# Loads of x and stores of the output rows in 112 and 15 partitions, or one strided transfer of 128 rows, in place of 127

## The chip, the cores and the metric

The kernel runs on one core of one Trainium2 chip. A core has TensorE (PE; PEld is its weight loading), VectorE (DVE), ScalarE (ACT), GpSimd (POOL) and SyncE (SP), on-chip memories SBUF and PSUM with 128 partitions each, and 16 DMA engines that move data between SBUF and the chip's main memory. The metric is the device time of one execution in microseconds, as the median of several runs. Lower is better.

## The reference, cut to what matters

```python
xn = layernorm(x)                                  # x: 6250 nodes x 256, f32; src, dst: 200000 edges
h = relu(xn[dst] @ W1 + b1); w = sigmoid(h @ W2 + b2)
gnn = segment_sum(xn[dst] * w, src) / segment_sum(w, src)
k, v = head_norm(xn, kln), head_norm(xn, vln)      # 8 heads of 32
mix = einsum(q=xn, kv=k.T @ v / N) + xn
x = x + gnn + mix
f = layernorm(x)
top2 of softmax(relu(f @ r1) @ r2) over 6 experts, each a 3-layer MLP of 256
return x + sum(top2 weight * expert(f))            # out_rows: 6250 x 256, f32
```

## The kernel before, in words

The 6250 nodes are laid out as 49 blocks (`BLOCKS`): node 49p + b is lane (partition) p of block b. 6250 is no multiple of 49, so lanes 0 to 126 (`LANES` = 127) have all 49 blocks and the last lane has only 27 (`SHORT`). In main memory the 49 rows of a lane lie side by side, 49 KB; the rows of one block lie 49 rows apart.

Opening. SyncE issues every plain DMA, from one queue in program order: first the edge arrays src and dst (125 partitions of 1600), then x in two parts (`X_PARTS`: blocks 0 to 20, blocks 21 to 48), each as a DMA of 127 partitions and one for the last lane (lines 494 to 498; part 1 behind a wait for VectorE's memset of the missing rows, `x_zeroed`), then 13 small weights and biases (L500 to L512) and six more. VectorE builds one sort key for each edge and runs a bitonic sort of 18 levels over them (L1399, L1407). Between its early passes it computes the statistics of x (L1369, L1373), part 0 after level 2, part 1 after level 3; it waits for `x_loaded[part]` there. GpSimd turns the statistics into scale and shift (L621 to L627). ScalarE then normalises blocks (L772, waiting for all small loads, x_loaded[0] and x_norm) and TensorE, ScalarE and GpSimd run 25 front rounds of two blocks each, in which GpSimd has the spread (L639 to L647). From level 8 on the sort needs TensorE's transposes (L1089); front rounds are placed between them.

Dense loop. After the sort a loop over the blocks builds for each destination block the counts of its edges by source (VectorE's one-hot marks, L1475; TensorE L1130; ScalarE's copy L927) in groups, two groups ahead, and multiplies them with the table of normalised rows (TensorE L1148). In the same round, spread over 28 steps, the six experts of the block two behind are computed (TensorE L1173, L1182, L1190; ScalarE L887), and the next block is normalised and routed. VectorE starts the output row block `y_acc` with L1586 in step 3 and adds one expert each time with L1593, the last in step 27. There is one `y_acc`. `store_all` on SyncE waits for the last add of block b, then stores it: for b < 27 with a DMA of lanes 0 to 126 and a second of the last lane, from 27 on with the first alone and a `nop` that adds the other 16 to `row_stored`. L1586 of the next block waits for `row_stored`, because it overwrites `y_acc`:

```python
if experts and j == places["begin"]:
    dve.wait_ge(S["row_stored"], 1 + 32 * n)
    dve.wait_ge(S["b3_ps"], n + 1)
    nc.vector.tensor_tensor(y_acc, x2, ps_b3, ALU.add)
```

VectorE executes in order, so whatever mark (L1475) comes behind L1586 waits with it. The last two blocks run without the building of counts (`ALONE`). A second path (`cut_flag`) repeats the aggregation in another way; it is not taken with these inputs.

Of the kernel before, what the change touches and what calls it, by code (L numbers as in the profile page):

```python
# [24 lines left out]
P = 128  # L25
NODES, DIM = 6250, 256
# [9 lines left out]
BLOCKS = -(-NODES // P)  # L36
# [3 lines left out]
LANES = NODES // BLOCKS  # L40
SHORT = NODES - LANES * BLOCKS
assert LANES == P - 1 and 0 < SHORT < BLOCKS

# [165 lines left out]
def gps_layer(nc, a, out, y_table, kept_keys):  # L211
    with ExitStack() as ctx:
# [7 lines left out]
        base = sb("base", [P, BLOCKS, DIM])  # L220
# [109 lines left out]
        x2, xn2, y_acc = after(DIM), after(DIM), after(DIM)  # L330
# [107 lines left out]
        S = {name: sem(name) for name in names}  # L438
# [38 lines left out]
        ordered = keys[exchanges_before(LEVELS + 1, LEVELS) % 2]  # L477
        assert ordered.shape == keys[1].shape

        node_rows = [t[0:LANES * BLOCKS, :].rearrange("(p t) d -> p t d", t=BLOCKS) for t in (a["x"], out)]  # L480
        last_rows = [t[LANES * BLOCKS:NODES, :].unsqueeze(0) for t in (a["x"], out)]
        kept_chunks = kept_keys[0:COLS, :].rearrange("(t p) q -> p t q", p=P)
        ordered_chunks = ordered.rearrange("p (t q) -> p t q", q=P)

# [3 lines left out]
        def _(sp):  # L488
# [2 lines left out]

            (at, to), (rest_at, rest_to) = X_PARTS
            assert to <= SHORT < rest_to
            sp.dma_start(base[0:LANES, at:to, :], node_rows[0][:, at:to, :]).then_inc(x_loaded[0], 16)
            sp.dma_start(base[LANES:P, at:to, :], last_rows[0][:, at:to, :]).then_inc(x_loaded[0], 16)
            sp.wait_ge(S["x_zeroed"], 1)
            sp.dma_start(base[0:LANES, rest_at:rest_to, :], node_rows[0][:, rest_at:rest_to, :]).then_inc(x_loaded[1], 16)
            sp.dma_start(base[LANES:P, rest_at:SHORT, :], last_rows[0][:, rest_at:SHORT, :]).then_inc(x_loaded[1], 16)

            sp.dma_start(gnn_w1[:, :, :], a["L0_gnn_W1"].rearrange("(h p) n -> p h n", p=P)).then_inc(S["small_loaded"], 16)  # L500
            sp.dma_start(gnn_b1[:, :], a["L0_gnn_b1"].rearrange("(p o) -> p o", o=1)).then_inc(S["small_loaded"], 16)
# [42 lines left out]
            def store_all(first):  # L544
                with sp.Fori(0, SHORT) as b:
                    sp.wait_ge(S["ey_added"], 1 + EXPERTS * (first + b + 1))
                    sp.dma_start(node_rows[1][:, bass.ds(b, 1), :], y_acc[0:LANES, :].unsqueeze(1)).then_inc(S["row_stored"], 16)
                    sp.dma_start(last_rows[1][:, bass.ds(b, 1), :], y_acc[LANES:P, :].unsqueeze(1)).then_inc(S["row_stored"], 16)
                with sp.Fori(SHORT, BLOCKS) as b:
                    sp.wait_ge(S["ey_added"], 1 + EXPERTS * (first + b + 1))  # L550
                    sp.dma_start(node_rows[1][:, bass.ds(b, 1), :], y_acc[0:LANES, :].unsqueeze(1)).then_inc(S["row_stored"], 16)
                    sp.nop().then_inc(S["row_stored"], 16)
                sp.wait_ge(S["row_stored"], 1 + 32 * (first + BLOCKS))

            store_all(0)
# [195 lines left out]
        def _(act):  # L751
# [9 lines left out]
                act.wait_ge(S["dst_lane_ready"], n + 1)  # L761
                nc.scalar.activation(dst_lane, dst_lane, ACT.Identity, bias=shift[0:LOAD_ROWS, :]).then_inc(S["dst_lane_ready"], 1)
            act.wait_ge(S["small_loaded"], 16 * N_SMALL)
            act.wait_ge(x_loaded[0], 32)
            act.wait_ge(S["x_norm"], 1)


# [44 lines left out]
            with nc.scalar.Fori(*FRONT_FIRST) as u:  # L812
                front_round(u)

            act.wait_ge(x_loaded[1], 32)
            act.wait_ge(S["x_norm"], 2)


# [482 lines left out]
        def _(dve):  # L1301
# [59 lines left out]

            def statistics(part):
                at, to = X_PARTS[part]
                dve.wait_ge(x_loaded[part], 32)
                dve.wait_ge(S["x_zeroed"], 1)
                per = 7
                with nc.vector.Fori(at // per, to // per) as t:
                    for k in range(per):
                        nc.vector.bn_stats(x_stats[:, per * t + k, :], base[:, per * t + k, :]).then_inc(S["x_stat"], 1)  # L1369

                dve.wait_ge(S["x_stat"], to)
                for t in range(at, to):
                    nc.vector.bn_aggr(x_mean_var[:, t, :], x_stats[:, t, :]).then_inc(S["x_stats_ready"], 1)  # L1373
# [364 lines left out]
```

## Time and profile before

| | us |
|---|---|
| median of 3 runs | 2786.89 (2786.73 to 2791.58) |
| profiled execution, own time | 2783.34 |
| its span on the core | 2781.6 |
| TensorE busy | 2196.4 (79%) |
| VectorE busy | 1760.5 (63%) |
| ScalarE busy | 1157.1 (42%) |
| GpSimd busy | 494.1 (18%) |
| DMA moved | 30.83 MB, mean 11 GB/s |

In the profile, times are microseconds from the start of the span, unless marked ns. A slice digit is the busy share in tenths of one fortieth of the span (70 us), 9 for 90% or more; PEclk is the TensorE clock granted, in tenths of 2.4 GHz, so that 5 is its lower level of 1.2 GHz. The chain that ended last is followed back from the last instruction: at each step to what released it. "SPq" is an issue on SyncE's queue. A stretch of the windows view lists the busy time of each engine in it with the number of instructions, then the granted clock, the mean busy share of the 16 DMA engines and what they moved.

### The profile page before, as it was taken

To read this page: it belongs to the slowest core of one execution; us is meant where nothing else is said; L and a number is where in the kernel's file an instruction comes from. 1 tells how busy PE (TensorE), PEld (TensorE's weight loads), DVE (VectorE), ACT (ScalarE), POOL (GpSimd) and SP (SyncE) were. 2 spreads that over 40 slices of the span, in tenths; PEclk is the share of its full clock that TensorE was granted. 3 is DMA by queue.
4 is the path that set the end of the run, shared out by engine and by line. 5 is a ranking of instruction groups with operands and counts; after the bars stand their busy time and mean duration, and the time that the engine had idled before them with its cause. 6 is when DMAs were issued, how large, how long until landed. Compare 5 with 4: busy or idle time off the path is not lost.

```text
span 2781.6 us, 53408 instructions
## 1 busy us (share of the span) xinstructions
PE 2196.4 (79%) x18096; PEld 1961.3 (71%) x18096; DVE 1760.5 (63%) x4212; ACT 1157.1 (42%) x2861; POOL 494.1 (18%) x414
## 2 busy tenths in 40 slices
PE   0002477654499999999999999999999999999997
PEld 0001366644388888888888888888888888888886
DVE  4203489899686666566666666666666666666662
ACT  0001234324444544444444454544445445444444
POOL 0001967778710000000000000000000000000000
PEclk9999677757699999999999999999999999999999
DMA  1000000001120000000000000000000000000000
GB/s 44 27 29 23 0 0 1 1 10 46 52 72 5 5 5 6 5 4 6 5 4 6 5 4 5 6 5 4 6 5 4 6 5 4 5 6 4 4 5 7
DMA packets 29005, 30.83 MB, mean 11 GB/s; under 512 B 7283, under 2 KB 26852, under 8 KB 28703
## 3 DMA queue, kind: packets, MB, share of 16 engines
q1 hardware_dynamic: 25758, 26.97, 2.9%
q0 software_dynamic: 3200, 3.28, 0.4%
q8 instruction: 23, 0.38, 0.1%
q14 instruction: 24, 0.20, 0.0%
HBM read 16.55 MB, written 13.70 MB: 11 GB/s over the span
## 4 chain that ended last, share of the span: by engine, by line
PE 55%; DMA 12%; issue 9%; POOL 8%; DVE 7%; another core or an unknown queue 7%; DVEq 1%; ACT 0%; SPq 0%; POOLq 0%; ACTq 0%
PE turned L1148 24%; DMA out_rows<-feat_mem 12%; PE front L1182 9%; PE front L1190 8%; PE front L1173 7%; PE turned L1130 4%; POOL acc_mem L639 4%; DVE sort_mem L1399 2%; DVE sort_mem L1475 2%; POOL tab_mem L625 1%; POOL sort_mem L701 1%; DVE feat_mem L1593 1%; PE front L1216 1%; DVE feat_mem L1586 1%
## 5 line engine op out<-in xcount | busy, mean ns | idle before, releaser
L1475 DVE TENSOR_TENSOR sort_mem<-lane_bf,sort_mem 128x512 bf16<-128x512 bf16 (+1 forms) x1372 | 829.5, 646 | 188.1 <-PE turned L1130 176.4
L1148 PE MATMUL turned<-acc_mem,sort_mem 128*128 128x257 bf16 x4998 | 707.7, 278 | 0.5 <-ACT sort_mem L935 0.5
L927 ACT ACTIVATE sort_mem<-turned 128x512 bf16<-128x512 f32 (+2 forms) x686 | 371.9, 542 | 486.7 <-PE turned L1130 486.6
L1148 PEld LDWEIGHTS turned<-acc_mem,sort_mem 128*128 128x128 bf16 x4998 | 486.3, 100 | 84.0 <-issue 0.5
L887 ACT ACTIVATE feat_mem<-front,b 128x128 f32<-128x128 f32 x1176 | 366.3, 363 | 380.2 <-PE front L1173 201.1
L715 POOL DMA_INDIRECT sort_mem<-kept_keys,key_at x100 | 110.4, 1104 | 1807.4 <-DVE key_at L1433 1791.7
L1399 DVE TENSOR_TENSOR sort_mem<-sort_mem 128x320 f32<-128x320 f32 (+2 forms) x568 | 345.7, 671 | 3.0
L1182 PE MATMUL front<-feat_mem 128*128 128x128 f32 x2352 | 337.9, 289 | 1.1 <-ACT feat_mem L887 1.1
L1130 PE MATMUL turned<-sort_mem 128*128 128x128 bf16 (+1 forms) x2695 | 247.4, 213 | 100.1 <-DVE sort_mem L1475 100.1
L1173 PE MATMUL front<-feat_mem 128*128 128x128 f32 x2352 | 322.4, 280 | 1.4 <-ACT feat_mem L887 1.4
L1182 PEld LDWEIGHTS front<-feat_mem 128*128 128x128 f32 x2352 | 298.9, 199 | 18.8 <-issue 15.6
L1190 PE MATMUL front<-feat_mem 128*128 128x256 f32 x1176 | 309.0, 385 | 1.4 <-DVE feat_mem L1593 1.3
L1130 PEld LDWEIGHTS turned<-sort_mem 128*128 128x128 bf16 x2695 | 195.6, 97 | 133.4 <-DVE sort_mem L1475 115.1
L1173 PEld LDWEIGHTS front<-feat_mem 128*128 128x128 f32 x2352 | 286.2, 192 | 3.6 <-ACT feat_mem L887 1.8
L1593 DVE SCALAR_TENSOR_TENSOR feat_mem<-front,feat_mem 128x256 f32<-128x256 f32 x294 | 141.6, 482 | 165.8 <-PE front L1190 151.7
L1012 PE MATMUL front<-ident,acc_mem 128*128 128x128 f32 x98 | 22.4, 371 | 262.8 <-ACT acc_mem L772 262.8
L1190 PEld LDWEIGHTS front<-feat_mem 128*128 128x128 f32 x1176 | 200.8, 191 | 18.4 <-DVE feat_mem L1593 2.5
L1012 PEld LDWEIGHTS front<-ident,acc_mem 128*128 128x128 f32 x98 | 16.8, 194 | 264.4 <-issue 256.8
L1148 PE MATMUL turned<-gath_mem,sort_mem 128*128 128x257 bf16 x1470 | 188.2, 273 | 0.0
L1148 PEld LDWEIGHTS turned<-gath_mem,sort_mem 128*128 128x128 bf16 x1470 | 143.4, 98 | 24.7
L1089 PE MATMUL turned<-ident,sort_mem 128*128 128x128 f32 x286 | 65.6, 405 | 99.9 <-DVE sort_mem L1399 97.9
L1369 DVE BATCH_NORM_STATS2 acc_mem<-base x49 | 16.2, 410 | 197.6 <-DMA base<-in_x 197.6
(217 smaller groups left out, 2358.0 us busy)
## 6 DMA issues: line engine op xcount, KB each, us to landing
gated_rows<-tab_mem SPq DMA_DIRECT2D x49, 128.5 KB, 2.3
out_rows<-feat_mem SPq DMA_DIRECT2D x49, 127.0 KB
feat_mem<-in_L_ffn_expert_w SPq DMA_DIRECT2D x18, 256.0 KB, 5.9
base<-in_x SPq DMA_DIRECT2D x1, 3556.0 KB
base<-in_x SPq DMA_DIRECT2D x1, 2667.0 KB
sort_mem<-kept_keys,key_at POOLq DMA_INDIRECT x100, 2.6
kept_keys<-sort_mem SPq DMA_DIRECT2D x1, 832.0 KB, 4.4
gath_mem<-in_src SPq DMA_DIRECT2D x1, 781.2 KB
```

The source lines that it names most:

```text
L639: nc.gpsimd.tensor_tensor(std[:, 0:heads], var[:, 0:heads], half_power[:, 0:heads], ALU.pow).then_inc(S["pool_step"], 1)
L715: nc.gpsimd.indirect_dma_start(out=window[:, half * P:(half + 1) * P], out_offset=None, in_=kept_keys, in_offset=bass.IndirectOffsetOnAxis ...
L887: nc.scalar.activation(sb_t[:, slot % 2, h, :], ps[:, h, :], ACT.Relu, bias=bias[:, slot, h:h + 1]).then_inc(ready, 1)
L927: nc.scalar.activation(a_tiles[:, k % 2, :, :].rearrange("p s n -> p (s n)")[:, 0:width], ps_a[k % 2][:, 0:width], ACT.Copy).then_inc(S["a ...
L1130: last = nc.tensor.matmul(ps_a[k % 2][:, at:at + width], hot_dst[:, k % 2, n, :], hot_src[:, k % 2, n, 0:width], start=True, stop=True)
L1148: last = nc.tensor.matmul(ps_agg, a_tiles[:, k % 2, n, :], y_part(t, part), start=(t == 0 and part == 0), stop=(t == BLOCKS - 1 and part = ...
L1173: last = nc.tensor.matmul(ps_h1[:, o, :], w1[:, e, h, o * P:(o + 1) * P], this_T[:, h, :], start=(h == 0), stop=(h == 1))
L1182: last = nc.tensor.matmul(ps_h2[:, o, :], w2[:, e, h, o * P:(o + 1) * P], h1_T[:, e % 2, h, :], start=(h == 0), stop=(h == 1))
L1190: last = nc.tensor.matmul(ps_y, h2_T[:, e % 2, h, :], w3[:, e, h, :], start=(h == 0), stop=(h == 1))
L1399: nc.vector.tensor_tensor(outs[t], lower, upper, ops[t]).then_inc(sorted_half[half], 1)
L1475: nc.vector.tensor_tensor(hot[:, k % 2, 0:count, 0:lanes], lane_bf[:, 0:lanes].unsqueeze(1).broadcast_to([P, count, lanes]), edge_tab[:, a ...
L1593: nc.vector.scalar_tensor_tensor(y_acc, ps_y, gates[:, e:e + 1], y_acc, ALU.mult, ALU.add).then_inc(S["ey_added"], 1)
```

## The change

Both loads of x go through `load_rows`, with three DMAs to a part: 112 partitions, 15 partitions, and the last lane as before; `x_loaded` is waited for with 48 in place of 32. The stores of blocks 0 to 26 become one DMA of 128 rows, 49 rows apart in main memory, and the `nop`; those of blocks 27 to 48 become two DMAs, of 112 and of 15 rows. Bytes, order and all other instructions stay.

```diff
--- before.py
+++ after.py
@@ -40,6 +40,7 @@
 LANES = NODES // BLOCKS
 SHORT = NODES - LANES * BLOCKS
 assert LANES == P - 1 and 0 < SHORT < BLOCKS
+LANE_PARTS = (slice(0, 112), slice(112, LANES))
 
 
 
@@ -477,8 +478,8 @@
         ordered = keys[exchanges_before(LEVELS + 1, LEVELS) % 2]
         assert ordered.shape == keys[1].shape
 
-        node_rows = [t[0:LANES * BLOCKS, :].rearrange("(p t) d -> p t d", t=BLOCKS) for t in (a["x"], out)]
-        last_rows = [t[LANES * BLOCKS:NODES, :].unsqueeze(0) for t in (a["x"], out)]
+        node_rows = a["x"][0:LANES * BLOCKS, :].rearrange("(p t) d -> p t d", t=BLOCKS)
+        last_rows = a["x"][LANES * BLOCKS:NODES, :].unsqueeze(0)
         kept_chunks = kept_keys[0:COLS, :].rearrange("(t p) q -> p t q", p=P)
         ordered_chunks = ordered.rearrange("p (t q) -> p t q", q=P)
 
@@ -491,11 +492,14 @@
 
             (at, to), (rest_at, rest_to) = X_PARTS
             assert to <= SHORT < rest_to
-            sp.dma_start(base[0:LANES, at:to, :], node_rows[0][:, at:to, :]).then_inc(x_loaded[0], 16)
-            sp.dma_start(base[LANES:P, at:to, :], last_rows[0][:, at:to, :]).then_inc(x_loaded[0], 16)
+            def load_rows(part, at, to):
+                for lanes in LANE_PARTS:
+                    sp.dma_start(base[lanes, at:to, :], node_rows[lanes, at:to, :]).then_inc(x_loaded[part], 16)
+                sp.dma_start(base[LANES:P, at:min(to, SHORT), :], last_rows[:, at:min(to, SHORT), :]).then_inc(x_loaded[part], 16)
+
+            load_rows(0, at, to)
             sp.wait_ge(S["x_zeroed"], 1)
-            sp.dma_start(base[0:LANES, rest_at:rest_to, :], node_rows[0][:, rest_at:rest_to, :]).then_inc(x_loaded[1], 16)
-            sp.dma_start(base[LANES:P, rest_at:SHORT, :], last_rows[0][:, rest_at:SHORT, :]).then_inc(x_loaded[1], 16)
+            load_rows(1, rest_at, rest_to)
 
             sp.dma_start(gnn_w1[:, :, :], a["L0_gnn_W1"].rearrange("(h p) n -> p h n", p=P)).then_inc(S["small_loaded"], 16)
             sp.dma_start(gnn_b1[:, :], a["L0_gnn_b1"].rearrange("(p o) -> p o", o=1)).then_inc(S["small_loaded"], 16)
@@ -544,12 +548,13 @@
             def store_all(first):
                 with sp.Fori(0, SHORT) as b:
                     sp.wait_ge(S["ey_added"], 1 + EXPERTS * (first + b + 1))
-                    sp.dma_start(node_rows[1][:, bass.ds(b, 1), :], y_acc[0:LANES, :].unsqueeze(1)).then_inc(S["row_stored"], 16)
-                    sp.dma_start(last_rows[1][:, bass.ds(b, 1), :], y_acc[LANES:P, :].unsqueeze(1)).then_inc(S["row_stored"], 16)
+                    sp.dma_start(out[bass.ds(b, P, BLOCKS), :], y_acc).then_inc(S["row_stored"], 16)
+                    sp.nop().then_inc(S["row_stored"], 16)
                 with sp.Fori(SHORT, BLOCKS) as b:
                     sp.wait_ge(S["ey_added"], 1 + EXPERTS * (first + b + 1))
-                    sp.dma_start(node_rows[1][:, bass.ds(b, 1), :], y_acc[0:LANES, :].unsqueeze(1)).then_inc(S["row_stored"], 16)
-                    sp.nop().then_inc(S["row_stored"], 16)
+                    for lanes in LANE_PARTS:
+                        rows = bass.ds(b + lanes.start * BLOCKS, lanes.stop - lanes.start, BLOCKS)
+                        sp.dma_start(out[rows, :], y_acc[lanes, :]).then_inc(S["row_stored"], 16)
                 sp.wait_ge(S["row_stored"], 1 + 32 * (first + BLOCKS))
 
             store_all(0)
@@ -761,7 +766,7 @@
                 act.wait_ge(S["dst_lane_ready"], n + 1)
                 nc.scalar.activation(dst_lane, dst_lane, ACT.Identity, bias=shift[0:LOAD_ROWS, :]).then_inc(S["dst_lane_ready"], 1)
             act.wait_ge(S["small_loaded"], 16 * N_SMALL)
-            act.wait_ge(x_loaded[0], 32)
+            act.wait_ge(x_loaded[0], 48)
             act.wait_ge(S["x_norm"], 1)
 
 
@@ -812,7 +817,7 @@
             with nc.scalar.Fori(*FRONT_FIRST) as u:
                 front_round(u)
 
-            act.wait_ge(x_loaded[1], 32)
+            act.wait_ge(x_loaded[1], 48)
             act.wait_ge(S["x_norm"], 2)
 
 
@@ -1361,7 +1366,7 @@
 
             def statistics(part):
                 at, to = X_PARTS[part]
-                dve.wait_ge(x_loaded[part], 32)
+                dve.wait_ge(x_loaded[part], 48)
                 dve.wait_ge(S["x_zeroed"], 1)
                 per = 7
                 with nc.vector.Fori(at // per, to // per) as t:
```

## Rows read from the trace of the kernel before

**Rows 1.** The page: chain that ended last, by engine and line, share of the span.
```profile
PE turned L1148 24%; DMA out_rows<-feat_mem 12%; PE front L1182 9%; PE front L1190 8%; PE front L1173 7%; PE turned L1130 4%; POOL acc_mem L639 4%; DVE sort_mem L1399 2%; DVE sort_mem L1475 2%; POOL tab_mem L625 1%; POOL sort_mem L701 1%; DVE feat_mem L1593 1%; PE front L1216 1%; DVE feat_mem L1586 1%
```

**Rows 2.** Timeline of the opening: start us, us, engine line op xcount [idle before].
```profile
15.41 0.99 DVE L1337 TENSOR_SCALAR acc_mem<-gath_mem 125x1600 f32<-125x1600 int32 x1 [4.51 <-DMA gath_mem<-in_dst]
...
38.51 2.09 DVE L1399 TENSOR_TENSOR sort_mem<-sort_mem 128x512 f32<-128x512 f32 x4
...
62.24 112.24 SPq L498 DMA_DIRECT2D base<-in_x  x1
117.84 6.96 DVE L1369 BATCH_NORM_STATS2 acc_mem<-base  x21 [77.24 <-DMA base<-in_x]
...
252.99 9.24 DVE L1369 BATCH_NORM_STATS2 acc_mem<-base  x28 [120.36 <-DMA base<-in_x]
...
255.45 1.09 ACT L772 ACTIVATE acc_mem<-base,tab_mem 128x256 f32<-128x256 f32 x2 [233.74 <-DMA b<-in_L_ffn_expert_b]
```

**Rows 3.** Stretches: busy PE, PEld, DVE, ACT, POOL; granted clock, DMA share, GB/s.
```profile
6.00:12.00 6.00, 0.00 (x0) 0.00 (x0) 4.25 (x14) 0.00 (x0) 0.00 (x0) 1.00 0.32 133
41.00:117.00 76.00, 0.00 (x0) 0.00 (x0) 0.00 (x0) 0.00 (x0) 0.00 (x0) 1.00 0.06 27
780.00:785.00 5.00, 5.00 (x56) 4.43 (x54) 3.78 (x9) 1.63 (x4) 0.00 (x0) 1.00 1.11 342
1427.00:1437.00 10.00, 7.90 (x57) 6.88 (x56) 8.89 (x20) 2.32 (x6) 2.13 (x2) 0.83 0.02 3
```

**Rows 4.** Waits from 812 to 2725 us: total us, times, longest us.
```profile
PE turned L1130 <- DVE sort_mem L1475: 93.9, 46, 2.2
PEld turned L1130 <- DVE sort_mem L1475: 106.9, 46, 2.4
...
DVE feat_mem L1586 <- DMA out_rows<-feat_mem: 152.1, 46, 4.6
```

**Rows 5.** Timeline of one block's stall, 1500 to 1512 us.
```profile
1501.95 0.23 SPq L547 DMA_DIRECT2D out_rows<-feat_mem  x1
...
1508.44 0.83 PE L1148 MATMUL turned<-acc_mem,sort_mem 128*128 128x257 bf16 x6
1509.51 0.42 DVE L1586 TENSOR_TENSOR feat_mem<-feat_mem,front 128x256 f32<-128x256 f32 x1 [3.36 <-DMA out_rows<-feat_mem]
...
1511.40 0.40 PE L1130 MATMUL turned<-sort_mem 128*128 128x128 bf16 x4 [2.13 <-DVE sort_mem L1475]
```

**Rows 6.** Chain in order of time, behind the stall: start us, us, what.
```profile
1512.75 1.34 PE turned L1148 x12
1514.08 0.22 PE turned L1130 x4
```

**Rows 7.** The page: DMA issues by tensors, KB each, us to landing.
```profile
gated_rows<-tab_mem SPq DMA_DIRECT2D x49, 128.5 KB, 2.3
...
base<-in_x SPq DMA_DIRECT2D x1, 3556.0 KB
base<-in_x SPq DMA_DIRECT2D x1, 2667.0 KB
```

**Rows 8.** Timeline of GpSimd before its first spread, and ScalarE's wait for it.
```profile
270.17 35.04 POOL L625 TENSOR_TENSOR tab_mem<-acc_mem,tab_mem 128x28 f32<-128x28 f32 x1
...
ACT acc_mem L799 <- POOL acc_mem L647: 69.3, 13, 39.6
```

**Rows 9.** Timeline of SyncE's stores, first ones and last ones of the loop.
```profile
847.92 0.27 SPq L547 DMA_DIRECT2D out_rows<-feat_mem  x1
848.41 1.07 SPq L548 DMA_DIRECT2D out_rows<-feat_mem  x1
...
968.81 0.23 SPq L547 DMA_DIRECT2D out_rows<-feat_mem  x1
...
2729.11 44.22 SPq L551 DMA_DIRECT2D out_rows<-feat_mem  x3
```

**Rows 10.** SyncE's queue, its waits from 2700 us.
```profile
SPq L557 <- DMA out_rows<-feat_mem: 6.7, 1, 6.7
```

## The prediction

> **What bounds the kernel now.** I read the page first, then the timeline of the opening, then one block of the long loop, then its waits. In the page the reader is to look at the chain that ended last [rows 1]: among TensorE's lines stands a transfer, the store of output rows, with 12% of the span. The page's slices send the reader to the opening as well, where TensorE has nothing to do.
>
> The timeline of the opening [rows 2] shows who is waited for. VectorE has its first keys at 15.41, sorts until 40.60, and then stands for 77.24 us until part 0 of x lands; after 15 us of work it stands again for 120.36 us until part 1 lands. Together 197.6 us, and nothing else runs meanwhile. ScalarE's first `norm` waits to 255.45 for the small weights, which SyncE could issue only after it had got rid of the x loads: the last of these took 112.24 us to issue, to 174.5.
>
> The stretches [rows 3] show what that transfer is. From 41 to 117 us the 16 DMA engines are busy to 0.06 (one sixteenth) and move 27 GB/s. So the 127-partition load runs on one engine. The two edge loads have 125 partitions, and while they run the share is 0.32, five sixteenths. The expert weights, of 128 partitions, reach 342 GB/s with the whole set busy (1.11).
>
> After the opening comes the sort with the front rounds (253 to 750 us), then 47 blocks of the dense loop from 812 us on. There TensorE is busy to nine tenths or more, and its only wait worth naming is for VectorE's marks, once in a block: 93.9 us over 46 times, 106.9 us on the weight-load side [rows 4]. VectorE in turn waits 152.1 us in that stretch for the store of the row before. One block shows the order [rows 5]: SyncE issues the store at 1501.95; VectorE is ready for `y_acc` = x2 + b3 at 1506.15, which may not overwrite the row being stored; it waits 3.36 us, to 1509.51, and only behind it stands the L1475 mark that TensorE could use at 1509.1 and gets at 1511.4.
>
> **The change, part by part.** The sum is made against the profiled execution's own 2783.34 us (span 2781.6).
>
> 1. *Loads of x.* The trace has no 112-partition load. Its nearest rows are 128 partitions (all 16 engines, 342 GB/s) and 125 (five engines, 133 GB/s with part of x beside it) [rows 3]. x is 6.4 MB (6250 rows of 1 KB; the rows of its two large DMAs [rows 7]), the edges 1.6 MB (200000 x 2 x 4 bytes). With 16 engines, 8.0 MB at 342 GB/s are 23 us; the engines that also carry the edges have some 0.72 MB each (0.32 + 0.40), at 342/16 = 21.4 GB/s that is 34 us. VectorE wants part 0 at 40.60, so both waits are gone: -77.24 - 120.36 = -197.6. With only five engines, part 0 (2.7 MB at 133 GB/s, behind the edges at 15.4) is there at 36 us and part 1 (3.6 MB) at 63; VectorE would want it at 55.4 (the 14.8 us from 117.84 to 252.99 - 120.36 after 40.60) [rows 2], so 8 us would be left. I take 16 engines, as 112 divides as 128 does; the bound costs 8 us. What this does to the edge loads: now all engines compete while they run. They got 26.6 GB/s an engine (133/5) and would get 21.4: 1.56 MB over five engines then take 15 us in place of 12. All of VectorE's work hangs on them, so 0 to +3; I take +1.5. The two added issues cost SyncE 0.27 us each [rows 9], and nothing behind them on its queue is urgent; part 1's are still behind the x_zeroed wait, on a memset that VectorE runs first of all.
>
> 2. *What is late next.* ScalarE needs x_norm(1) and the small loads. Before, these took from 174.5 to 255.45, 81 us, queued behind the x loads; now they are issued from about 10 us on, and even if they took 81 us again ScalarE would start at 91 where the mere shift gives 255.45 - 197.6 = 57.9. That lateness would cost nothing: GpSimd must do the norm of part 1 first, and its L625 is held for 35.04 us, to 305.2, while VectorE sorts without a break; ScalarE waits 39.6 us in one piece for the spread behind it [rows 8], so it may come up to 39 us later than 57.9, to 97. For the same reason an earlier start earns nothing. The orders of VectorE and GpSimd are unchanged, so I move this whole stage by 197.6. Its TensorE clock alternates between both levels, which may shift it by some 5 us either way (my choice; no row gives it).
>
> 3. *Stores.* For b < 27 one DMA of 128 rows in place of 127 + 1; from 27 on two, of 112 and 15. The nearest row is the store of 128.5 KB from 128 partitions, landed 2.3 us after issue, against some 7.5 us from the issue at 1501.95 to VectorE's start at 1509.51 [rows 5, 7]. Two stores of a pair are issued 0.49 us apart [rows 9], so the pair lands after some 3 us, at 1505. VectorE reaches L1586 at 1506.15: the wait of 3.36 us vanishes wholly. From the other side: L1130 starts 1.9 us behind L1586 (1509.51 to 1511.40), so L1586 may start as late as 1507.2 and a store of 5.2 us costs nothing either. TensorE comes to L1130 without idling at 1508.44 + 0.67 = 1509.11 (half of the 1.34 that twelve L1148 take in the chain), and four L1130 in flow take 0.22 [rows 6]: done at 1509.33, where it was 1511.80: 2.47 us. The two wait rows give 2.04 and 2.32 a block. I take 2.4; 46 blocks are -110.4 (bounds -93.9 and -113.6). Behind the waiting L1586 nothing else is queued that is late, and next on the line is TensorE's own stream: VectorE's and ScalarE's later work stands at the same distance to TensorE as now.
>
> The Trainium skill, *DMA: Bandwidth & Descriptors*, in "Why a DMA increments its semaphore by 16 and not by 1", says that a DMA runs on the largest number of engines up to 16 that divides its outermost size. The shares 0.06 and 0.32 agree with its 1 for 127 and 5 for 125; By it 112 gets 16 and 15 gets 15, and the sum stands as it is; by the row of 125 alone it would be the five-engine bound, 8 us more. The same page's "Rules for kernel authors" speaks against the change: two transfers to disjoint partition ranges serialise, better use one. By it the split gives nothing; that is rival C.
>
> 4. *Clock.* In a regular block the stores are 40.30 us apart ((968.81 - 847.92)/3), yet from the first to the 47th it is (2729.11 - 847.92)/46 = 40.90 [rows 9]. The difference is the clock: after some stalls the granted clock falls to 1.2 GHz for a moment. From 1427 to 1437 it is 0.83 in the mean [rows 3], in a stretch in which TensorE had just stood idle for its 2 us. Without the stall it has no cause: -0.60 x 46 = -27.5.
>
> 5. *End.* In the last two blocks L1586 waits for its store too, but there the expert layers of TensorE and ScalarE run beside it; I give that nothing (bound: the two waits of 48 - 46 blocks, some 2 us each). The last store is waited for with 6.7 us [rows 10] and needs 2.3 to 2.8: -4.2.
>
> Sum: 2783.34 - 197.6 + 1.5 - 110.4 - 27.5 - 4.2 = 2445.1. The runs shown have a median 3.5 us above that execution; for the new kernel 0 to 3.5 of this may come; I add 0.9: **2446 us**.
>
> **Rivals.**
> - *B, the clock keeps falling.* If the drops have another cause than the stall, 27.5 us come back: 2474. For it: most stalls bring none, so the stall alone does not make one. Against: the one shown comes right behind a stall, and elsewhere in the loop TensorE waits for nobody [rows 4].
> - *C, the split halves serialise* (the rule above), so each pair runs as the one did, on one engine. The loads stay at 27 GB/s; only the 27 stores of 128 rows in one DMA gain: 27 x (2.4 + 0.6) = 81 less, 2702; if that strided store stays on one engine as well, the change does not do what it says: 2786, no difference.
> - *D, TensorE gets no gain from the store*, because another mark or ScalarE's copy becomes late in its place. Load side and end alone: 2783.34 - 197.6 + 1.5 - 4.2 = 2583. Against: no other TensorE wait in the rows of the loop.
> - *E, slower.* The packets stay on one engine and the second DMA of the pair is issued 0.49 us later and takes 1.07 us to issue: in 22 blocks VectorE waits 0.49 to 1.07 us longer [rows 9], and TensorE, which has no slack behind that wait, passes it all on: +11 to +24, 2800. It decides from the point where 112 lanes take as long as 127. The share 0.32 for 125 partitions speaks against it.
> - *F, part of the opening stays:* five engines for the loads and the edges 3 us late, +8 + 1.5, and the stall worth the lesser bound, +16.5: 2472.
>
> **How the numbers follow.** Forecast 0.74 (its own range 2434 to 2460, from the bounds of the stall, the edges and the sort's clock), B 0.08, F 0.07, D 0.04, C 0.04 (half of it without effect), E 0.03. The range 2432 to 2476 takes in B and F and leaves out C, D, E and some of the forecast's own tails. Within 0.2% (5.6 us, about what a measurement of this kernel tells from no change) lies only the half of C and the near end of E: 0.03; slower 0.02; faster 0.95.
>
> **What would show it.** After: VectorE's idle time before L1369 near 0 in place of 197.6; in the first 35 us DMA shares near 1; first L772 between 55 and 91; POOL L639 first at about 108; no wait of L1586 for out_rows in the loop, and no wait of TensorE's L1130 for L1475; stores 37.9 us apart, all alike; granted clock 1.00 through the loop; the share of out_rows in the chain below 1%. It would be wrong if x landed in a 15-partition tail on one engine after 55 us, if 112 ran on few engines in the stores, or if the sort stage, given its data early, ran longer.

## The result, and the profile after

The changed kernel takes 2455.64 us in the median of 4 runs (2451.41 to 2462.77), against 2786.81 for the kernel before (2786.44 to 2791.58): a ratio of 0.8811, 95% interval 0.8788 to 0.8834. Forecast were 2446 and 2432 to 2476. The profiled execution took 2454.61 us, its span 2452.9.

In the page after, the reader should look at TensorE's slices (work begins in the second slice, not the fourth, and the loop is full), at the clock, which leaves its full level only before the loop, and at the chain, in which the store of output rows no longer appears (12% before, [rows 1]). Lines 494 and on have moved by up to six: L1591 is what was L1586, L1480 was L1475, L1135 was L1130, L1374 was L1369, L644 was L639.

```profile
PE   0276774546999999999999999999999999999998
...
DVE  6949989987767667677676676766767767667662
...
PEclk9677776778999999999999999999999999999999
DMA  6000000113000000000000000000000000000000
...
PE turned L1153 32%; PE front L1187 11%; PE front L1178 11%; PE front L1195 11%; PE turned L1135 5%; POOL acc_mem L644 4%; DVE sort_mem L1404 2%; POOL tab_mem L630 1%; PE front L1205 1%; POOL sort_mem L706 1%; DMA gath_mem<-in_dst 1%; PE front L1221 1%; POOL acc_mem L710 1%; PE front L1226 1%; POOL acc_mem L708 0%
```

The opening, from the timeline. It answers to [rows 2]: no idle time stands before either group of statistics. But the keys begin at 26.25 and not at 15.41, and their wait for the edge arrays is now 15.35 us long in place of 4.51.

```profile
26.25 0.99 DVE L1342 TENSOR_SCALAR acc_mem<-gath_mem 125x1600 f32<-125x1600 int32 x1 [15.35 <-DMA gath_mem<-in_dst]
...
49.33 2.09 DVE L1404 TENSOR_TENSOR sort_mem<-sort_mem 128x512 f32<-128x512 f32 x4
51.34 6.95 DVE L1374 BATCH_NORM_STATS2 acc_mem<-base  x21
...
66.04 9.23 DVE L1374 BATCH_NORM_STATS2 acc_mem<-base  x28
...
66.75 1.09 ACT L777 ACTIVATE acc_mem<-base,tab_mem 128x256 f32<-128x256 f32 x2 [34.21 <-POOL tab_mem L632]
```

GpSimd before its first spread, for [rows 8]: L630 is held for as long as before, 35.03 us, and L644 starts at 118.79 in place of 305.75.

```profile
83.21 35.03 POOL L630 TENSOR_TENSOR tab_mem<-acc_mem,tab_mem 128x28 f32<-128x28 f32 x1
...
118.79 3.08 POOL L644 TENSOR_TENSOR acc_mem<-acc_mem,gath_mem 128x16 f32<-128x16 f32 x1
```

Stretches, in the columns of [rows 3]. The DMA engines are all busy (1.01 to 1.04) until 30 us, but move 187 to 243 GB/s. In the loop, TensorE is busy for 300.00 of 300 us and its clock stays at 1.00.

```profile
6.00:12.00 6.00, 0.00 (x0) 0.00 (x0) 4.24 (x14) 0.00 (x0) 0.00 (x0) 1.00 1.03 243
12.00:20.00 8.00, 0.00 (x0) 0.00 (x0) 0.00 (x0) 0.00 (x0) 0.00 (x0) 1.00 1.01 187
20.00:30.00 10.00, 0.00 (x0) 0.00 (x0) 3.65 (x4) 3.66 (x3) 0.00 (x0) 1.00 1.04 230
30.00:40.00 10.00, 0.00 (x0) 0.00 (x0) 9.83 (x7) 2.51 (x2) 0.00 (x0) 1.00 0.66 123
1450.00:1750.00 300.00, 300.00 (x2666) 271.08 (x2665) 210.81 (x541) 154.50 (x393) 17.07 (x16) 1.00 0.02 5
```

The last of these stretches in the kernel before, where TensorE is busy for 285.16 us at a mean clock of 0.98:

```profile
1450.00:1750.00 300.00, 285.16 (x2481) 255.29 (x2480) 192.89 (x502) 145.20 (x370) 14.95 (x14) 0.98 0.02 5
```

The stores. The view of one line gives the issues and the time from issue to landing: 1.7 us in every case for the single DMA of 128 rows, and 1.7 us in the median (1.5 at the least) for those of 112 and 15 rows together. For [rows 9], the first store of the loop and the 47th: they are (2405.01 - 658.38)/46 = 37.97 us apart, in place of 40.90.

```profile
L551 SPq DMA_DIRECT2D out_rows<-feat_mem x27: 332/333/364, 658.4 to 1645.7; - x27
...
DMA to landing us min/median/max: 1.7/1.7/1.7
...
L557 SPq DMA_DIRECT2D out_rows<-feat_mem x44: 316/332/830, 1683.6 to 2449.2; - x44
...
DMA to landing us min/median/max: 1.5/1.7/2.4
```

```profile
658.38 987.64 SPq L551 DMA_DIRECT2D out_rows<-feat_mem  x27
...
2405.01 45.05 SPq L557 DMA_DIRECT2D out_rows<-feat_mem  x6
```

For [rows 10], SyncE's wait for the last store is 1.4 us where it was 6.7:

```profile
SPq L562 <- DMA out_rows<-feat_mem: 1.4, 1, 1.4
```

For [rows 4] there is next to nothing to show: from 620 to 2405 us TensorE's matmuls wait for nobody, its weight loads wait once for a mark of L1480, for 0.2 us, and VectorE's waits have no entry for out_rows.

### The profile page after: what moved, and what is told of

It is laid out like the page before. It is cut to its first block, busy times and chain, and to the rows that moved or that the text cites. A ratio compares the mean times of both kernels' runs of the same rounds, so it can differ in the third digit from the quotient of the medians.

```text
span 2452.9 us, 53400 instructions
## 1 busy us (share of the span) xinstructions
PE 2152.1 (88%) x18096; PEld 1938.2 (79%) x18096; DVE 1756.7 (72%) x4212; ACT 1157.1 (47%) x2861; POOL 493.7 (20%) x414
## 4 chain that ended last, share of the span: by engine, by line
PE 76%; POOL 9%; issue 8%; DVE 5%; DMA 1%; ACT 0%; DVEq 0%; POOLq 0%; SPq 0%; ACTq 0%
PE turned L1153 32%; PE front L1187 11%; PE front L1178 11%; PE front L1195 11%; PE turned L1135 5%; POOL acc_mem L644 4%; DVE sort_mem L1404 2%; POOL tab_mem L630 1%; PE front L1205 1%; POOL sort_mem L706 1%; DMA gath_mem<-in_dst 1%; PE front L1221 1%; POOL acc_mem L710 1%; PE front L1226 1%; POOL acc_mem L708 0%
## 5 line engine op out<-in xcount | busy, mean ns | idle before, releaser
L1480 DVE TENSOR_TENSOR sort_mem<-lane_bf,sort_mem 128x512 bf16<-128x512 bf16 (+1 forms) x1372 | 829.4, 646 | 188.1 <-PE turned L1135 176.2
L1153 PE MATMUL turned<-acc_mem,sort_mem 128*128 128x257 bf16 x4998 | 690.1, 274 | 0.5 <-ACT sort_mem L940 0.5
L1153 PEld LDWEIGHTS turned<-acc_mem,sort_mem 128*128 128x128 bf16 x4998 | 476.3, 98 | 75.2 <-issue 0.5
L1187 PE MATMUL front<-feat_mem 128*128 128x128 f32 x2352 | 322.8, 280 | 1.1 <-ACT feat_mem L892 1.1
L1178 PE MATMUL front<-feat_mem 128*128 128x128 f32 x2352 | 322.4, 280 | 1.4 <-ACT feat_mem L892 1.4
L1187 PEld LDWEIGHTS front<-feat_mem 128*128 128x128 f32 x2352 | 285.5, 191 | 18.8 <-issue 15.6
L1178 PEld LDWEIGHTS front<-feat_mem 128*128 128x128 f32 x2352 | 286.2, 192 | 3.6 <-ACT feat_mem L892 1.8
L1135 PE MATMUL turned<-sort_mem 128*128 128x128 bf16 (+1 forms) x2695 | 245.4, 212 | 6.2 <-DVE sort_mem L1480 6.2
L1135 PEld LDWEIGHTS turned<-sort_mem 128*128 128x128 bf16 x2695 | 198.4, 97 | 27.4 <-DVE sort_mem L1480 8.3
L1195 PEld LDWEIGHTS front<-feat_mem 128*128 128x128 f32 x1176 | 200.8, 191 | 17.9 <-DVE feat_mem L1598 2.1
L1094 PEld LDWEIGHTS turned<-ident,sort_mem 128*128 128x128 f32 x286 | 50.7, 205 | 109.7 <-DVE sort_mem L1404 106.4
L644 POOL TENSOR_TENSOR acc_mem<-acc_mem,gath_mem 128x16 f32<-128x16 f32 (+1 forms) x25 | 99.3, 3973 | 79.2 <-ACT acc_mem L806 79.2
L1434 DVE TENSOR_SCALAR_CACHE_REDUCE tab_mem<-tab_mem,thr 64x1664 uint8<-64x1664 f32 x50 | 96.8, 1937 | 12.3 <-DVE feat_mem L1522 12.2
```

Source lines behind the costliest of these rows:

```text
L644: nc.gpsimd.tensor_tensor(std[:, 0:heads], var[:, 0:heads], half_power[:, 0:heads], ALU.pow).then_inc(S["pool_step"], 1)
L1094: last = nc.tensor.transpose(turned[:, at:at + P], held[:, at:at + P], ident[:, :])
L1135: last = nc.tensor.matmul(ps_a[k % 2][:, at:at + width], hot_dst[:, k % 2, n, :], hot_src[:, k % 2, n, 0:width], start=True, stop=True)
L1153: last = nc.tensor.matmul(ps_agg, a_tiles[:, k % 2, n, :], y_part(t, part), start=(t == 0 and part == 0), stop=(t == BLOCKS - 1 and part = ...
L1178: last = nc.tensor.matmul(ps_h1[:, o, :], w1[:, e, h, o * P:(o + 1) * P], this_T[:, h, :], start=(h == 0), stop=(h == 1))
L1187: last = nc.tensor.matmul(ps_h2[:, o, :], w2[:, e, h, o * P:(o + 1) * P], h1_T[:, e % 2, h, :], start=(h == 0), stop=(h == 1))
```

## The experiments

Each was timed beside the kernel before, in four runs where nothing else is said; the kernel before had medians of 2785.4, 2787.0 and 2786.8 us on those occasions.

**1. The loads alone.** The stores are as before, 127 and 1.

```diff
-                    sp.dma_start(out[bass.ds(b, P, BLOCKS), :], y_acc).then_inc(S["row_stored"], 16)
-                    sp.nop().then_inc(S["row_stored"], 16)
+                    sp.dma_start(out_node_rows[:, bass.ds(b, 1), :], y_acc[0:LANES, :].unsqueeze(1)).then_inc(S["row_stored"], 16)
+                    sp.dma_start(out_last_rows[:, bass.ds(b, 1), :], y_acc[LANES:P, :].unsqueeze(1)).then_inc(S["row_stored"], 16)
```

> Only the loads of x are changed, the stores are those of before (127 and 1). Theory: the two halves of the change add up. The opening gives back 187 us (197.6 less the 10.8 that the edges now come later) and 2 to 3 more in the sort, the loop stays 40.9 us a block with its drops of the clock: 2786.8 - 190 = 2597. Rival (the stall of the loop is a child of the late opening, so the halves overlap): under 2560.

Measured: 2599.71 us, ratio 0.9324 (0.9302 to 0.9346). The timeline of VectorE shows the late edges and no wait for x; the stretch of the loop shows TensorE's pauses and a clock of 0.98, as in the kernel before:

```profile
26.35 0.99 DVE L1343 TENSOR_SCALAR acc_mem<-gath_mem 125x1600 f32<-125x1600 int32 x1 [15.45 <-DMA gath_mem<-in_dst]
...
51.44 6.94 DVE L1375 BATCH_NORM_STATS2 acc_mem<-base  x21
```

```profile
1450.00:1750.00 300.00, 283.04 (x2442) 252.73 (x2441) 195.14 (x498) 142.58 (x362) 17.08 (x16) 0.98 0.02 5
```

**2. The stores alone.** x is loaded with 127 partitions and 1, as before.

```diff
-            load_rows(0, at, to)
+            sp.dma_start(base[0:LANES, at:to, :], node_rows[:, at:to, :]).then_inc(x_loaded[0], 16)
+            sp.dma_start(base[LANES:P, at:to, :], last_rows[:, at:to, :]).then_inc(x_loaded[0], 16)
             sp.wait_ge(S["x_zeroed"], 1)
-            load_rows(1, rest_at, rest_to)
+            sp.dma_start(base[0:LANES, rest_at:rest_to, :], node_rows[:, rest_at:rest_to, :]).then_inc(x_loaded[1], 16)
+            sp.dma_start(base[LANES:P, rest_at:SHORT, :], last_rows[:, rest_at:SHORT, :]).then_inc(x_loaded[1], 16)
```

> Only the stores are changed, the loads of x are those of before. Theory: the opening stays (edges at 15.4, VectorE 197.6 us idle before its statistics), the loop goes at 38.0 us a block with the granted clock at 1.00 throughout, the end is 4.6 shorter: 2786.8 - 134.6 - 4.6 = 2648. Rival (the drops of the clock do not come from the stall): 40.9 - 2.4 = 38.5 a block, 2675.

Measured: 2645.02 us, ratio 0.9503 (0.9476 to 0.9529). The edges are on time, the wait for part 0 of x is back, and the loop runs without a pause at full clock:

```profile
15.55 0.99 DVE L1339 TENSOR_SCALAR acc_mem<-gath_mem 125x1600 f32<-125x1600 int32 x1 [4.65 <-DMA gath_mem<-in_dst]
...
118.17 6.96 DVE L1371 BATCH_NORM_STATS2 acc_mem<-base  x21 [77.45 <-DMA base<-in_x]
```

```profile
1450.00:1750.00 300.00, 300.00 (x2666) 271.23 (x2666) 208.32 (x535) 156.39 (x396) 17.14 (x16) 1.00 0.02 5
```

The two halves save 185.7 and 140.4 us, together 326.1; the whole change saved 331.2. So they add up within the scatter, and neither needs the other. The clock's drops went with the stores, not with the opening: between the first and the 47th store the granted clock falls 20 times in the kernel before, 21 times with the loads alone, and never with the stores alone.

**3. The edges spread as well**, in 112 and 13 partitions (the two waits for them are adapted).

```diff
-            sp.dma_start(src_in[0:LOAD_ROWS, :], ...)
-            sp.dma_start(dst_in[0:LOAD_ROWS, :], ...)
+            for rows in (slice(0, 112), slice(112, LOAD_ROWS)):
+                for edge_in, name in ((src_in, "src"), (dst_in, "dst")):
+                    sp.dma_start(edge_in[rows, :], a[name].rearrange("(p c) -> p c", p=LOAD_ROWS)[rows, :]).then_inc(S["edges_loaded"], 16)
```

> The changed kernel, with the edge arrays too loaded in 112 and 13 partitions in place of 125. Theory: the edges came late because they ran on five engines that all sixteen slowed down; on all engines, ahead of x in the queue, 1.6 MB land by 10 us, VectorE begins the keys at about 11 (its other work ends at 10.9) in place of 26.25, and x still lands before VectorE asks for it at 36: 2455.6 - 15.3 = 2440. Rival (the memory, not the number of engines, holds the edges up, so they still come with x at 22 to 26): 2451 to 2456.

Measured: 2448.16 us, ratio 0.8777 (0.8745 to 0.8809). The keys begin at 10.82, without a wait, and x is there when it is asked for at 35.89 and 50.60:

```profile
10.82 0.98 DVE L1343 TENSOR_SCALAR acc_mem<-gath_mem 125x1600 f32<-125x1600 int32 x1
...
35.89 6.95 DVE L1375 BATCH_NORM_STATS2 acc_mem<-base  x21
...
50.60 9.23 DVE L1375 BATCH_NORM_STATS2 acc_mem<-base  x28
```

So the mechanism holds (five engines, and not the memory, kept the edges waiting), and the price does not: 15.4 us earlier in the opening, 7.5 in the median. In the profiled run the stretch from GpSimd's first spread to the first store was 549.7 us long, against 539.6 in the changed kernel.

**4. x issued after the edges have landed.**

```diff
+            sp.wait_ge(S["edges_loaded"], 32)
             load_rows(0, at, to)
```

> The changed kernel, with SyncE waiting for both edge arrays before it issues the loads of x; the edges stay on their five engines. Theory: the edges land at 15.4 or a little earlier again, part 0 of x at about 30, part 1 at about 46, before VectorE asks at 40 and 55: 2455.6 - 10.8 = 2445. Rival (x is then late itself): part of the gain is eaten by an idle stretch before the statistics, 2450 to 2465.

Measured: 2445.16 us, ratio 0.877 (0.8751 to 0.8789).

```profile
15.55 0.99 DVE L1343 TENSOR_SCALAR acc_mem<-gath_mem 125x1600 f32<-125x1600 int32 x1 [4.66 <-DMA gath_mem<-in_dst]
...
40.64 6.95 DVE L1375 BATCH_NORM_STATS2 acc_mem<-base  x21
...
55.35 9.23 DVE L1375 BATCH_NORM_STATS2 acc_mem<-base  x28
```

With nothing beside them the edges land as in the kernel before, and x is still early enough. The 10.7 us are the price of the competition, 26.25 against 15.55.

**5. 125 and 2 partitions** in place of 112 and 15, in loads and stores.

```diff
-LANE_PARTS = (slice(0, 112), slice(112, LANES))
+LANE_PARTS = (slice(0, 125), slice(125, LANES))
```

> The changed kernel with 125 and 2 partitions in place of 112 and 15, in the loads and in the 22 stores of two. Theory: 125 runs on five engines; the edges, first in the same five queues, land at 15.5 again; part 0 of x lands by 36 to 40, part 1 near 63 where VectorE asks at 55, so about 8 us idle; a store of 25 rows to an engine is 1 us longer, hidden. 2455.6 - 10.8 + 8 = 2453. Rival (how many engines is not what counts, any split does the same as 112 and 15): edges at 26, no wait for x, 2455.6. The two differ in the trace, not in the time.

Measured: 2462.72 us, ratio 0.8828 (0.8794 to 0.8861).

```profile
15.61 0.99 DVE L1342 TENSOR_SCALAR acc_mem<-gath_mem 125x1600 f32<-125x1600 int32 x1 [4.71 <-DMA gath_mem<-in_dst]
...
40.70 6.95 DVE L1374 BATCH_NORM_STATS2 acc_mem<-base  x21
...
67.41 9.24 DVE L1374 BATCH_NORM_STATS2 acc_mem<-base  x28 [11.93 <-DMA base<-in_x]
```

```profile
6.00:12.00 6.00, 0.00 (x0) 0.00 (x0) 4.24 (x14) 0.00 (x0) 0.00 (x0) 1.00 0.37 144
20.00:30.00 10.00, 0.00 (x0) 0.00 (x0) 9.83 (x8) 1.87 (x2) 0.00 (x0) 1.00 0.31 129
40.00:50.00 10.00, 0.00 (x0) 0.00 (x0) 9.96 (x46) 0.00 (x0) 0.65 (x2) 1.00 0.34 139
```

The DMA share is 0.31 to 0.37, five engines, and stays so through the loads. The edges land at 15.61, although x stands in the queue right behind them: what delays them in the changed kernel is the traffic of the eleven other engines. Part 1 is 11.93 us late where 8 was expected, which is 1.3 us more than the edges gain, so GpSimd's first spread comes at 120.16 in place of 118.79. The median is 7.1 us above that of the changed kernel, where the theory had it 2.6 below; the sort stage of the profiled execution was 4.2 us longer, which is within its scatter (see the last section), and the intervals of the two ratios overlap.

**6. Stores one after the other**, to lengthen the landing while every DMA stays spread over many engines: two, three, four and five DMAs to a row block, each issued when the one before has landed (the counts that SyncE and VectorE wait for are adapted). The packets tell the spread: of a piece of 32 rows up to 13 are under way at once, of one of 16 rows up to 7, and of the old store of 127 rows never more than 2. The edit for four:

```diff
+                def in_turn(b, parts):
+                    for n, (at, to) in enumerate(parts):
+                        if n:
+                            sp.wait_ge(S["row_stored"], 1 + 64 * (first + b) + 16 * n)
+                        sp.dma_start(out[bass.ds(b + at * BLOCKS, to - at, BLOCKS), :], y_acc[at:to, :]).then_inc(S["row_stored"], 16)
...
+                    in_turn(b, ((0, 32), (32, 64), (64, 112), (112, P)))
```

> The changed kernel with each output row block stored as two DMAs, the second issued only when the first has landed (112, then the other 16 or 15 lanes): about 4.3 us from issue to landing in place of 1.7 to 2.4. Theory (up to 5.2 us are hidden by VectorE's own work): no change, 2455.6, blocks 38.0 us apart. Rival (every us of landing costs): blocks up to 2 us longer, 2550.

> As the one of two in turn, with three (48, 64, 16 or 15 lanes): about 6.4 us. Theory: 1.2 us over what is hidden, TensorE idle 1.2 us in each of 46 blocks, 2455.6 + 55 = 2510, perhaps without a drop of the clock as the gap is short. Rival (only the number of engines counts, all 16 are in use): 2456.

> As before, with four in turn (32, 32, 48, 16 or 15 lanes): about 8.5 us, longer than the store of the kernel before (7.5). Theory: TensorE idle 3.3 us in a block and the drops of the clock are back: 2455.6 + 152 + 28 = 2635. Rival for the clock (the drops belonged to the one busy engine of the old store): 2608 and a granted clock of 1.00 in the loop.

> As the one with four in turn, with five (32, 32, 32, 16, 16 or 15 lanes), all of them on 15 or 16 engines. From two, three and four in turn, a part adds 1.5 us: VectorE waits 2.4 + 1.5 = 3.9 us, a little more than in the kernel before (3.36), and TensorE stands idle 1.25 us less than that, 2.7. Theory: the drops of the clock are back, about one in two or three blocks, though the DMA is spread: 2528 + 46 x 1.5 + 28 = 2625. Rival (the drops belonged to the one busy engine of the old store, or to the late opening): the granted clock stays 1.00 in the loop, 2597.

Measured: two in turn 2460.25 us (four runs from 2451.95 to 2468.2), three 2471.68, four 2528.23, five 2616.5 us. VectorE's start of the output row in two successive blocks of three in turn, then of four, then of five, each with the stretch around it where it matters:

```profile
1429.08 0.42 DVE L1594 TENSOR_TENSOR feat_mem<-feat_mem,front 128x256 f32<-128x256 f32 x1 [1.26 <-DMA out_rows<-feat_mem]
...
1467.25 0.42 DVE L1594 TENSOR_TENSOR feat_mem<-feat_mem,front 128x256 f32<-128x256 f32 x1 [1.26 <-DMA out_rows<-feat_mem]
```

```profile
1456.86 0.42 DVE L1594 TENSOR_TENSOR feat_mem<-feat_mem,front 128x256 f32<-128x256 f32 x1 [2.44 <-DMA out_rows<-feat_mem]
...
1496.21 0.42 DVE L1594 TENSOR_TENSOR feat_mem<-feat_mem,front 128x256 f32<-128x256 f32 x1 [2.44 <-DMA out_rows<-feat_mem]
...
1450.00:1750.00 300.00, 290.56 (x2569) 260.61 (x2568) 204.23 (x522) 150.68 (x381) 17.08 (x16) 1.00 0.02 5
```

```profile
1445.84 0.42 DVE L1594 TENSOR_TENSOR feat_mem<-feat_mem,front 128x256 f32<-128x256 f32 x1 [3.91 <-DMA out_rows<-feat_mem]
...
1486.66 0.42 DVE L1594 TENSOR_TENSOR feat_mem<-feat_mem,front 128x256 f32<-128x256 f32 x1 [3.90 <-DMA out_rows<-feat_mem]
...
1528.78 0.42 DVE L1594 TENSOR_TENSOR feat_mem<-feat_mem,front 128x256 f32<-128x256 f32 x1 [3.90 <-DMA out_rows<-feat_mem]
...
1300.00:1600.00 300.00, 281.38 (x2475) 252.71 (x2475) 192.49 (x499) 145.59 (x368) 14.97 (x14) 0.99 0.02 5
```

| kernel | VectorE's wait, us | regular block, us | TensorE's clock in the loop |
|---|---|---|---|
| changed kernel | 0 | 37.97 | 1.00 |
| two in turn | 0 | 37.98 | 1.00 |
| three in turn | 1.26 | 38.17 | 1.00 |
| four in turn | 2.44 | 39.35 | 1.00 (one drop, in the first block) |
| kernel before | 3.36 [rows 5] | 40.30 | 0.98 |
| five in turn | 3.90 | 40.82 | 0.99 |

From 1.26 us of waiting on, each further microsecond costs a microsecond in the block, and the old kernel with its one busy engine stands on the line of those whose stores are spread: 38.17 + (3.36 - 1.26) = 40.27 against 40.30. So it is the time to landing that counts, and the number of engines only through it. About 1.06 us of VectorE's waiting are free (38.17 - 37.97 = 0.20 of 1.26 are paid). The clock: from 700 us on, with four in turn TensorE pauses 46.8 us in 41 of the blocks, 1.1 us each, and the clock stays at full level. In the first block of the loop its pause is 2.07 us long, and there the clock does fall, at 671. With five it pauses 108.9 us in 42, 2.6 each, and drops are back, in 8 of the 46 blocks. The block from 1486.66 to 1528.78 is one of them, 42.12 us long in place of 40.82. This rules out the old engine and, with experiments 1 and 2, the late opening as their cause.

The forecasts for three and four in turn were too high, since a further part adds 1.2 to 1.5 us to VectorE's wait and not 2.1, and since the drops expected with four stayed away but for the one. That for five was 8.5 us too high: fewer blocks have a drop than the one in two or three that it assumed.

**7. Part 0 of x as one DMA of 128 partitions** (one round), on top of experiment 4. Lane 127 has its rows 0 to 20 where the stride would put them, so one transfer can take them all.

```diff
-            load_rows(0, at, to)
+            rows_of_all = bass.AP(tensor=a["x"].tensor, offset=a["x"].offset, ap=[[BLOCKS * DIM, P], [1, to * DIM]])
+            sp.dma_start(base[:, 0:to, :].rearrange("p t d -> p (t d)"), rows_of_all).then_inc(x_loaded[0], 48)
```

> The kernel that waits for the edges before it loads x, with part 0 of x as one DMA of 128 partitions in place of 112, 15 and 1. Theory (lane counts that are no multiple of 128 spread well, but move less: 222 to 255 GB/s here against 342 for the weights): part 0 alone, from 17 us on, moves at over 300 GB/s and is in by 26. Rival (the rows of 21 KB, or reading x, give 250 whatever the split): 220 to 260 GB/s in that stretch too. The time does not change in either case (VectorE asks at 40.6): 2445.

Measured: 2446.23 us (two runs, 2441.15 and 2451.31), no different in time from experiment 4. The stretch from 18 to 24 us, in which nearly all packets are of part 0, first with 128 partitions, then with 112, 15 and 1 (the repeat of experiment 4):

```profile
18.00:24.00 6.00, 0.00 (x0) 0.00 (x0) 5.90 (x5) 3.74 (x3) 0.00 (x0) 1.00 1.07 434
```

```profile
18.00:24.00 6.00, 0.00 (x0) 0.00 (x0) 5.90 (x5) 3.59 (x3) 0.00 (x0) 1.00 0.99 247
```

The theory held: part 0 moves at over 300 GB/s and its last packet ends at 25.0. Its packets are of 21504 bytes in both kernels, so their size is not the difference: one takes 0.80 us in the first and 1.38 us in the second. In the first kernel too the rate falls when part 1 is under way, which is still split in 112, 15 and 1 (some small loads run beside it):

```profile
24.00:28.00 4.00, 0.00 (x0) 0.00 (x0) 3.93 (x3) 0.00 (x0) 0.00 (x0) 1.00 0.97 237
```

**8. Experiments 3 and 4 again**, with five runs of each.

> The kernel with the edges in 112 and 13 partitions once more, beside the one below on the same chip. In its profile the keys began at 10.82, 15.4 us before those of the changed kernel, but the sort stage behind took 550 us where that of the changed kernel took 540. Theory (the length of the sort stage scatters by 10 us from run to run in every version, and the gain is real): median 2440, 15 below the changed kernel and some 5 below the one that waits for the edges. Rival (the sort stage gives it back): 2448 again, no better than the one that waits.

> The kernel that loads x after the edges, once more. Theory and rival both: 2445, keys at 15.5.

Measured: edges spread 2445.92 us (2437.28 to 2458.06), ratio 0.878 (0.8753 to 0.8807); x after the edges 2450.99 (2442.49 to 2452.17), ratio 0.8791 (0.8772 to 0.8811). The one is 4.5 us earlier in its keys (10.82 against 15.36), and in the two profiled executions the stretch from the first spread to the first store is equally long (537.5 and 538.5 us) and the times, 2437.28 and 2442.49, keep the difference. But the theory's median of 2440 was missed, and the medians of all nine runs of each, 2446.3 and 2446.4, do not differ. Both are some 9 us under the changed kernel's 2455.64, the best that was found; the intervals of their ratios overlap with that of the changed kernel, so the trace's 10.7 us carry this claim more than the medians do.

## Why the prediction was right, step by step

**The two waits for x: right, with a wrong rate.** Both are gone, 197.6 us. The reason given, that 112 partitions run on all engines, is shown by the shares of 1.01 to 1.04. The rate taken for it, 342 GB/s from a load of 128 partitions, was too high: 187 to 243 were moved. All of x was to be in by 34 us; the last packets of part 0 and part 1 ended at 38.3 and 49.5. The slack covered the error, with little to spare for part 0: VectorE would have wanted it at 40.60 by the forecast, and asked at 51.34 because the edges were late. The bound of five engines, 8 us late, was 11.93 in the trace (experiment 5).

**The edges: the term that was mis-sized.** Forecast 0 to +3, taken +1.5; measured 26.25 - 15.41 = +10.84. The step that failed is "they got 26.6 GB/s an engine and would get 21.4". From 6 to 12 us all engines together moved 243 GB/s, 15.2 an engine. At that rate 1.6 MB on five engines take 21 us. Experiments 3, 4 and 5 take the cause away in three ways, and each time the keys start at 10.8 or 15.6.

**The stage behind moves as a block: right, within its scatter.** L639 was to start at about 108 by a shift of 197.6; with the edges' delay it is 119, and it was 118.79. ScalarE's first L777 came at 66.75, in the range given, and it mattered to nobody, since GpSimd's own chain (L626 to L632, without a gap) sets the start of the first spread. From the first spread to the first store the changed kernel took 539.6 us where the old took 542.2. The 5 us of play that I chose for this stage were too few: the same stretch was 530.4 with the stores alone and 549.7 in experiment 3.

**The stall: right.** L1591 has no wait for out_rows in the loop, L1135 none for L1480. Forecast 2.4 us a block, measured 40.30 - 37.97 = 2.33, so -107.2 in place of -110.4. One reading behind the 2.4 was off: the prediction lets TensorE reach L1130 at 1509.11, by the chain's mean for L1148, but [rows 5] has that work done at 1508.44 + 0.83 = 1509.27, which makes 2.31 of its 2.47, nearer to what was measured. The landing took 1.7 us for a single store, less than the 2.3 of the nearest row. The free play of 1.06 us (experiment 6) agrees with the forecast's 5.2 us to a landing that costs nothing: 1507.2 less 1506.15.

**The clock: right.** Forecast -27.5; the old loop has 40.90 in the mean and 40.30 in a regular block, the new one 37.97 in both. The regular block was taken from the first three. Over all 46, the old loop has 26 blocks without a drop, 40.19 us in the mean, and 20 with one, 41.82. Counted so, the stall is worth 102.0 us and the drops 32.6; the forecast had the sum (137.9, measured 134.6) better than its two parts. Rival B falls: with the stores alone no drop is left.

**The end: right.** Forecast -4.2; from the last store of the loop to the end of the span it was 52.5 us before and is 47.9, so -4.6.

Against 2783.34 the parts measured give -187.0 (opening, 305.75 to 118.79), -2.6 (sort), -134.6 (loop, 1881.19 to 1746.63), -4.6 (end): 2454.5, and the execution took 2454.61. The forecast was 9.6 us low in the median; the edges alone are 9.3 (10.84 - 1.5), and the rest nearly cancels, which is luck, as the sort stage alone scatters by more.

Of the rivals, C (the halves serialise on one engine) fell with the DMA shares. The Trainium skill, *DMA: Bandwidth & Descriptors*, "Rules for kernel authors", warns against splitting a transfer into partition halves, because both halves use the same engines anyway. That ground is not given here, where the unsplit transfer runs on one engine (27 GB/s [rows 3]), so the row does not decide this case. What the same page says of the number of engines, in "Why a DMA increments its semaphore by 16 and not by 1", fits every case seen: shares of about 1 for 112 and 15 together, and 0.31 to 0.37 for 125; 15 alone was not seen. D fell, as TensorE's matmuls have no wait in the loop. E fell with the landing of 1.7 us. F's edges were real and larger than there.

## What to carry to other kernels

Look at the DMA share of a large transfer beside its rate: one sixteenth means one engine, and a partition count of 127 or 125 can be the reason; split off a remainder so that the main part has a multiple of 16. Then ask what the faster transfer now competes with: the loads that VectorE waited for first were slowed by it, and cost more than any other error of the sum; what is needed first should be spread too, or have the engines to itself. A store between two uses of one buffer costs only what its landing exceeds the work in between, and that can be measured by landing it in pieces.

## What the runs showed of the hardware that was not expected

- A spread over all engines is not full rate. The same part 0 of x moved at 434 GB/s as one DMA of 128 partitions and at 247 GB/s as 112, 15 and 1, with shares of 1.07 and 0.99. The packets are of the same size, 21504 bytes, and take 1.38 us in place of 0.80. Why they do was not tried.
- DMAs that wait in order behind another on its own five engines do not delay it (keys at 15.61 with 125 and 2), traffic on the others does (26.25).
- TensorE's granted clock fell in the loop only at the end of a pause. In the kernel before, all 20 drops between the first and the 47th store begin from 0.1 us before to 0.9 us after TensorE resumes from a pause of 1.9 to 2.1 us, and such a block is 1.6 us longer. But most pauses bring none, and longer ones brought fewer: 8 drops in 46 blocks with pauses of 2.5 to 3.3 us (five in turn). With four in turn, 45 pauses of 1.0 to 1.5 us brought none, and the single one of 2.07 us brought one. What decides which pause brings a drop was not settled.
- The sort stage varies from run to run: 530 to 550 us from the first spread to the first store, in kernels whose instructions are the same there. In it TensorE's clock alternates between both levels. GpSimd can also be held elsewhere: in the run with the loads alone it was the first of its instructions for part 1 (the L627 there) that took 40.89 us beside VectorE's sort, where it was the third that took 35 us in all others, and the first spread began at 124.07 in place of 118.8. What decides either was not settled; it is the larger part of the scatter of the new kernels, and hides a gain of 5 us.
